# Decayed x of two units on ScalarE, and the next sequence's first norm applied over four steps

## The reference, cut to what matters

```python
x = x + _L0_attn_ref(_layernorm(x, axis=-1), ...)        # the mixer, with its norm

# inside: 32 heads of 64 columns, state of 128
def step(h, inp):
    dA_t, dt_t, x_t, B_t, C_t = inp
    u = (dt_t[:, :, None] * x_t)[..., None] * B_t[:, :, None, :]
    h = dA_t[:, :, None, None] * h + u
    y = jnp.einsum('bhpn,bhn->bhp', h, C_t)
    return (h, y)
...
y = jnp.moveaxis(ys, 0, 1) + D_param[None, None, :, None] * xs
g = y * _silu(gate)
g = g * jax.lax.rsqrt(jnp.mean(g * g, axis=-1, keepdims=True) + EPS) * norm_w
return jnp.einsum('bli,di->bld', g, W_out)
```

## Time and profile before

| | us |
|---|---|
| median of 3 runs | 1318.38 (1317.02 to 1319.73) |
| the profiled execution | 1316.61 |
| its span, first to last instruction | 1314.8 |
| TensorE busy | 1118.4 (85%) |
| VectorE busy | 884.8 (67%) |
| ScalarE busy | 656.9 (50%) |
| GpSimd busy | 555.9 (42%) |

### The profile page before, as it was taken

How to read it: one execution, slowest core, us unless ns; L and a number is a source line. 1 busy time by engine, 2 the same in 40 slices (tenths; PEclk the granted TensorE clock), 3 DMA queues, 4 the chain that set the end, 5 groups by cost and what they waited for, 6 DMA issues and landing times.

```text
span 1314.8 us, 24377 instructions
## 1 busy us (share of the span) xinstructions
PE 1118.4 (85%) x8378; PEld 722.3 (55%) x8380; DVE 884.8 (67%) x1850; ACT 656.9 (50%) x1575; POOL 555.9 (42%) x725
## 2 busy tenths in 40 slices
PE   2799998898999988989999988989999879877940
PEld 2355566665555556655555566655555556653520
DVE  4477886565878875657877875657777766662427
ACT  3655524666555525657554335666555245621630
POOL 0255661220387751210777821201777712143760
PEclk9899999899999999999999998999999999988975
DMA  8366553300253314101433323002433544077888
GB/s 325 105 213 190 183 176 77 97 2 21 91 161 114 113 47 108 50 4 35 145 124 117 104 77 94 5 22 65 144 110 114 187 109 145 2 257 239 159 199 323
DMA packets 120137, 159.56 MB, mean 121 GB/s; under 512 B 11632, under 2 KB 82928, under 8 KB 119280
## 3 DMA queue, kind: packets, MB, share of 16 engines
q1 hardware_dynamic: 106384, 131.73, 32.5%
q0 software_dynamic: 9216, 19.98, 5.8%
q10 hardware_dynamic: 4416, 6.29, 1.3%
HBM read 104.55 MB, written 40.83 MB: 111 GB/s over the span
## 4 chain that ended last, share of the span: by engine, by line
PE 47%; DVE 19%; ACT 12%; issue 9%; POOL 7%; DMA 4%; SPq 0%; POOLq 0%; DVEq 0%; ACTq 0%
PE bank L1187 10%; DVE pool_c L1690 6%; PE bank L1229 5%; PE bank L1110 4%; ACT joint L851 3%; PE bank L1410 3%; PE bank L1367 3%; PE bank L1395 3%; PE bank L1332 2%; ACT pool_c L812 2%; POOL joint L2200 2%; PE bank L1223 2%; PE bank L1497 2%; PE bank L1208 2%; PE bank L1216 2%
## 5 line engine op out<-in xcount | busy, mean ns | idle before, releaser
L1187 PE MATMUL bank<-xm,joint 128*128 128x512 f32 x544 | 269.1, 619 | 18.6 <-DVE pool_c L1690 12.9
L2200 POOL TENSOR_TENSOR joint<-joint 128x512 f32<-128x512 f32 x128 | 163.9, 1282 | 208.2 <-DVE joint L1706 205.1
L1690 DVE SCALAR_TENSOR_TENSOR pool_c<-bank,params,pool_c 128x511 f32<-128x511 f32 (+2 forms) x216 | 161.4, 748 | 95.9 <-ACT pool_c L812 90.0
L1187 PEld LDWEIGHTS bank<-xm,joint 128*128 128x128 f32 x544 | 98.5, 195 | 122.1 <-issue 92.2
L1891 DVE TENSOR_REDUCE nmax<-bank 128x1 f32<-128x384 f32 (+3 forms) x176 | 109.6, 637 | 60.6 <-PE bank L1368 59.8
L1229 PE MATMUL bank<-wout,pool_c 128*128 128x256 f32 x512 | 121.8, 381 | 3.4 <-DVE pool_c L1731 3.4
L851 ACT ACTIVATE joint<-bank,dt_ 128x64 f32<-128x64 f32 x512 | 111.7, 342 | 22.4 <-PE bank L1110 22.2
L1229 PEld LDWEIGHTS bank<-wout,pool_c 128*128 128x128 f32 x512 | 95.7, 190 | 36.1 <-issue 21.7
L2194 POOL DMA_INDIRECT xslot<-xrow,slots x96 | 96.0, 1000 | 26.7 <-issue 22.0
L821 ACT ACTIVATE pool_c<-pool_c 128x512 f32<-128x512 f32 x64 | 40.3, 630 | 116.4 <-DVE pool_c L1690 116.4
L977 ACT ACTIVATE pool_c<-bank 128x512 f32<-128x512 f32 (+1 forms) x156 | 83.2, 551 | 18.0 <-PE bank L1397 15.6
(11 more groups left out here) (272 smaller groups left out, 2361.6 us busy)
## 6 DMA issues: line engine op xcount, KB each, us to landing
pool_b<-dA_rows SPq DMA_DIRECT2D x64, 256.0 KB, 3.4
pool_b<-dec_rows SPq DMA_DIRECT2D x96, 128.0 KB, 3.6
joint<-pool_b SPq DMA_DIRECT2D x96, 128.0 KB, 2.4
acc<-xrow SPq DMA_DIRECT2D x13, 640.0 KB, 6.2
joint<-dA_rows SPq DMA_DIRECT2D x32, 256.0 KB
dA_late<-dA_rows SPq DMA_DIRECT2D x32, 256.0 KB
joint<-acc SPq DMA_DIRECT2D x32, 256.0 KB, 6.8
xslot<-xrow SPq DMA_DIRECT2D x16, 321.0 KB, 5.1
```

Source lines behind the costliest of these rows:

```text
L1187: last = mm(bank[:, :], win[:, k, col:col + P], xm[:, k, :], start=(k == 0), stop=(k == KD - 1))
L1690: ins = v.scalar_tensor_tensor(out=cv[:, n:L], in0=bank[:, 0:L - n], scalar=convw[:, ci, TAPS - 1 - n:TAPS - n], in1=cv[:, n:L], op0=ALU.m ...
L2200: M_ready.inc(p.tensor_tensor(M[u % 2][:, hs_, :], Lx[:, hs_, :], cbm[:, c * P:(c + 1) * P].unsqueeze(1).to_broadcast([P, 4, P]), ALU.mult))
```

## The change

Units 13 and 14 (`SCALED_BY_ACT`) get their decayed x from ScalarE. A new function `decayed_x(u)` waits for both scan halves of the unit, for x * dt and for the state product that read the same buffer last, and issues eight scaled copies of 128 x 64, one for each head. It is called at the start of ScalarE's step u - 1, ahead of `squares`. GpSimd leaves its one instruction (128 x 512) out for these two units. And `norm_apply` for the coming sequence runs for tile 0 in step 9, tile 1 in step 10, tile 2 in step 11 and tile 3 in step 12, at the end of VectorE's step.

```diff
+        SCALED_BY_ACT = (UNITS - 3, UNITS - 2)
...
+            def decayed_x(u):
+                c, g = u % T, u // T
+                at(L_ready, 2 * u + 2)
+                at(xdt_ready, GK * (g + 1))
+                at(ds_mm, grown(u - 1))
+                for h in range(GH):
+                    cols = slice(h * HP, (h + 1) * HP)
+                    ins = sa.activation(xde[u % 2][:, cols], xdt[g % 2][:, c, cols], ACT.Copy, scale=Lx[:, h, P - 1:P])
+                xde_ready.inc(ins)
...
                     first, early, late, last = ahead_of(s)
+                    if s + 1 in SCALED_BY_ACT:
+                        decayed_x(s + 1)
                     if s >= 1:
                         squares(s - 1)
...
-                    if coming is not None and HEAD_AT <= s <= HEAD_AT + T:
+                    if coming is not None and HEAD_AT <= s < HEAD_AT + T + 2:
                         row(coming)
                         if s == HEAD_AT:
                             dve.wait_ge(xnext_loaded.sem, xnext_loaded.upto(coming + 1))
                         if s < HEAD_AT + T:
                             norm_stats(0, s - HEAD_AT)
-                        else:
-                            for t in range(T):
-                                norm_apply(0, t)
+                        if s >= HEAD_AT + 2:
+                            norm_apply(0, s - HEAD_AT - 2)
                         row(here)
...
-                    if c < T - 1:
+                    if c < T - 1 and u not in SCALED_BY_ACT:
                         at(xdt_ready, GK * (g + 1))
```

## The result

The changed kernel takes 1340.5 us (median of 4 runs, 1336.32 to 1340.91) against 1317.97 for the kernel before, measured beside it: 22.5 us slower by the medians. The ratio of the two is 1.0157 with a 95% interval of 1.0141 to 1.0174, or 18.6 to 22.9 us. The forecast was 11.3 us slower, 1325 to 1336. The direction and the place were right; the size was half of what came, and the time lies outside the range.

The account below looks back on a forecast made before the run. Bound taken: the chain of waits through TensorE, VectorE and GpSimd in each sequence's tail. Sequence 0 +3.3, sequences 1 and 2 +2.6 each, sequence 3 +2.8: +11.3 us on 1318.4 gives 1329.7, range 1325 to 1336.

Parts of the forecast that it names:

- What bounds the kernel, and where the change acts: Steps 12 to 15: VectorE's scans of units 14 and 15 wait 0.66 and 0.45 us for GpSimd's decayed x.
- The square behind the eight: Steps 12 and 13: late square delays sum of squares, state product, state update and scan; +1.54 and +1.22 us, last sequence.
- The price of the eight: ScalarE, steps 12 and 13: eight copies take 1.57 us to the square, from a row of like copies reading PSUM.
- ceiling side: Upper side of the range: eight copies at 2.13 us, half way to their ceiling of 2.69, adding 4.5 us.
- The fourth application: VectorE, step 12, sequences 0 to 2: it stands between state update and scan of unit 14, costing 0.5 us.
- What step 11 gives back: VectorE, step 11: moving norm applications away gains 0.65 us in each of sequences 1 and 2, nothing in sequence 0.
- step 14: Step 14 has no eight copies, so TensorE catches up before VectorE's state update; nothing was put there.
- The clock: Rival, chance 0.08: TensorE idles in each tail and falls towards half clock, 12 us in all, about 1341 us.
- Faster: Rival, chance 0.05: square 11 done before TensorE reaches its sum of squares, scans follow state updates; 3.6 us saved, 1314.8.
- Same: Rival, chance 0.06: the delay is made but given back later by a stage that waits anyway; about 1319 us.

Follow-up runs that it names:

- e1: Changed kernel with ScalarE's squares ahead of the eight copies in steps 12 and 13: 1317.95 us against 1319.32 for the kernel before, ratio 0.9999.
- e5: Changed kernel with TensorE's state product ahead of the sum of squares in steps 12 and 13: 1325.7 us against 1318.88 for the kernel before.
- e6: Kernel before, with ScalarE waiting for both scan halves ahead of its square in steps 12 and 13, no eight copies: 1319.14 us against 1318.88.
- e7: Changed kernel, its eight copies reading PSUM scaled by Lx in step 12, and SBUF scaled by the dt column in step 13: one run, 1340.41 us.
- e2: Changed kernel with unused matmuls filling TensorE's wait before the sum of squares, 11 in step 12 and 14 in step 13: 1334.88 us, ratio 1.0118.
- e8: Changed kernel with squares ahead of the eight copies and the four norm applications back in step 11: 1316.6 us against 1318.88 for the kernel before.
- e3: Changed kernel with the four norm applications back in step 11, so only ScalarE's decayed x is changed: 1339.02 us, ratio 1.0155 to the kernel before.
- e4: Kernel before with one norm application in each of steps 9 to 12, decayed x still on GpSimd: 1318.94 us against 1319.32.

## Why the prediction was wrong in size

**What bounds the kernel, and where the change acts: right.** 21.3 us of the loss are in the tails, made in the two steps that I named, and the chain of waits and idle times that I read there are those that moved.

**The square behind the eight: right.** Sum of squares waits for ScalarE, state update for the state product, scan for VectorE's own work, in both steps. e1, e5 and e6 show each link by itself: place on ScalarE, place on TensorE, and that the wait alone is free.

**The price of the eight: mis-sized.** I took 1.57 us because form, width and number agreed with the row. The source didn't, and it is 1.92 from SBUF: 0.35 in each of eight steps, +2.8 us. My ceiling side (2.13) covered it. My estimate from the figures of the Trainium skill ("ScalarE: Activation LUTs", section "What ACT_TABLE_LOAD costs") was 1.91 us; the trace agrees for SBUF with 1.92, and doesn't for PSUM with 1.58 (e7).

**The fourth application: slightly too dear.** I took 0.5 us. It moves the scan behind it by 0.32, as VectorE's rows of sequence 0 show (184.61 to 184.93, L1679 the application):

```profile
184.61 0.41 DVE L1679 TENSOR_SCALAR pob<-pob,hmv,hrstd 128x256 f32<-128x256 f32 x1
184.93 1.21 DVE L1719 TENSOR_TENSOR_SCAN joint<-joint,bank 128x512 f32<-128x512 f32 x1
```

That is -0.5 us over three sequences. With both terms mended the tails go from my 12.6 (the sum without what step 11 gives back) to 14.9, and e2, where the clock holds, has 14.8. So the steps are complete as far as the queues go, step 14, in which I put nothing, included.

**What step 11 gives back: right, and small.** I put 0.65 us in sequences 1 and 2. From the start of the application to the second scan half it was 3.95 us before; it is 3.34 now (462.28 to 465.62), 0.61 less. In the time of the whole sequence it can't be found.

**The clock: the step that failed.** The forecast's sum has no term for it: it prices every product behind the waits at full clock. I left the fall to a rival at 0.08, since TensorE would be busy for 5.7 of 7.9 us in a step, nearer to the stretch that kept its clock. That share was a mean over a step and says nothing of the single wait inside it, which I put at 2.3 us and which lasted 2.6 to 3.3. In the last sequence the clock fell before the wait was over, in the others 0.5 to 1.6 us into the work behind it. It costs 1.1 to 2.7 us once in a tail, 6.5 in all, against the rival's 3 us in each of four. The rival's time, 1341, is all but the measured one, and yet its sum is not: it had 11.3 + 12, the runs show 14.8 + 6.5. My range left this case out by its chance. That the time came out near the rival's is in part luck: its clock was nearly twice as dear as measured and its queue order too cheap. The prices alone, 2.3 us more, would take my 1329.7 to 1332.0, inside the range; the clock's 6.5 take it on to 1338.5, past the end at 1336.

**The other rivals.** Faster was the outcome with the square out of the way: e8's tails gain 4.75 us, 1.19 in each, where I had 1.28 without the norm's application. The point that I named, the square ending before TensorE reaches the sum of squares, is what decides. Same: nothing shows that the tails' 21.3 us were given back later; the total's 18.6 to 22.9 includes them.

**What stays open.** About 3 us of the 24.3 between the two profiled spans lie outside the tails. No cause for them is shown or needed: runs of one kernel differ by up to 7.8 us, and the stretch behind the last tail, which no edit changes, takes from 272.3 to 277.3 us over the ten profiled kernels. Open, too, is which of the waits brings the clock down: in sequences 2 and 3 it was the one of step 12 (2.57 and 2.56 us), in sequences 0 and 1 that of step 13 (3.27 each), though step 12 had waited 2.57 and 2.56 there too. The length of the wait alone doesn't decide: in e3, sequence 1, one of 3.16 us in step 12 left the clock at 1.00. No run was made to find out what does.

## What to carry to other kernels

When work moves to an idle engine, look at what stands behind it in that engine's queue and who waits for that: here a square with 1.7 us of slack got eight cheap copies, with a wait of their own, put in front of it, and the same copies one place later cost nothing that the total shows. Price an operation by a row with the same source memory, and where a change opens a wait in TensorE's chain, add a term for the clock that the next products may run at.

## What the runs showed of the hardware

Eight scaled copies of 128x64 back to back on ScalarE take 1.92 us to the next start when they read SBUF and 1.58 when they read PSUM, whatever column scales them (e7).

Waits of 2.6 to 3.3 us on TensorE, within a stretch in which it was busy otherwise, brought 0.50 of the clock in one place of each tail, during the wait or up to 1.6 us behind it. The other waits of this length did not, nor did those of 2.29 us (e7), 1.70 and 1.89 (e5) or 1.06 (e6). Filling the waits with matmuls of no use held it at 1.00 (e2) and was worth 6.5 us in the tails. The Trainium skill ("TensorE: Matmul & The Clock Gate", section "What's actually happening") says that activity is what lifts TensorE from half clock; e2's rows agree.

A product of two operands in SBUF on VectorE takes 0.67 us alone and 3.10 beside three instructions of GpSimd's in a row (e4). In sequence 1 of the changed kernel it took 2.10 beside two, which cost nothing, since VectorE waited for TensorE afterwards; in e1 the same 2.09 is on the path.
